# Two of four probability tiles transposed by VectorE and a trip through memory instead of TensorE

## The reference, cut to what matters

```python
        q = rmsnorm((hidden_states @ Wq).reshape(B, Sq, H, D), gq)      # H = 16 heads, D = 128
        k = rmsnorm((encoder_hidden_states @ Wk).reshape(B, Skv, H, D), gk)
        v = (encoder_hidden_states @ Wv).reshape(B, Skv, H, D)
        scores = jnp.einsum('bqhd,bkhd->bhqk', q, k) * scale
        attn = jax.nn.softmax(scores, axis=-1)                          # 512 x 512 for each (b, h)
        out = jnp.einsum('bhqk,bkhd->bqhd', attn, v)
        out = out.reshape(B, Sq, H * D) @ Wo
```

## Time and profile before

| What | us |
|---|---|
| Runs shown | 1462.48, 1463.65 (median), 1465.13 |
| Span of the profiled execution | 1461.5 |
| PE busy in that span | 1437.8 (98%) |
| DVE / ACT / POOL busy | 1107.0 / 977.5 / 864.5 |
| Packed steps, from the first y store to the last | 517.7 to 1223.0, 31 stores |

### The profile page before, as it was taken

How to read it: one execution, slowest core, us unless ns; L and a number is a source line. 1 busy time by engine, 2 the same in 40 slices (tenths; PEclk the granted TensorE clock), 3 DMA queues, 4 the chain that set the end, 5 groups by cost and what they waited for, 6 DMA issues and landing times.

```text
span 1461.5 us, 23763 instructions
## 1 busy us (share of the span) xinstructions
PE 1437.8 (98%) x8086; PEld 1223.0 (84%) x8086; DVE 1107.0 (76%) x2100; ACT 977.5 (67%) x2224; POOL 864.5 (59%) x701
## 2 busy tenths in 40 slices
PE   8999999999999999999999999999999999999998
PEld 6778788888888888888888888888888888888887
DVE  7888777777777777777777777777777776787777
ACT  7864477777776667667676767667676765666664
POOL 4785555555554566666575757575666655664341
PEclk9999999999999999999999999999999999999999
DMA  8420011111111333434333433433434331321002
GB/s 325 159 66 16 22 44 45 57 44 44 44 44 44 139 124 126 149 108 147 124 129 127 139 123 127 139 117 132 136 115 144 125 126 36 107 82 37 8 1 87
DMA packets 55495, 142.74 MB, mean 98 GB/s; under 512 B 5392, under 2 KB 5392, under 8 KB 55376
## 3 DMA queue, kind: packets, MB, share of 16 engines
q1 hardware_dynamic: 51616, 128.90, 26.1%
q0 software_dynamic: 3760, 12.32, 3.0%
HBM read 126.79 MB, written 14.42 MB: 97 GB/s over the span
## 4 chain that ended last, share of the span: by engine, by line
PE 82%; DVE 7%; ACT 4%; POOL 4%; issue 2%; DMA 0%; ACTq 0%; SPq 0%; DVEq 0%; POOLq 0%
PE w_bank L505 10%; PE w_bank L507 10%; PE w_bank L506 10%; PE j_bank L505 9%; PE j_bank L507 9%; PE j_bank L506 9%; PE t_bank L573 7%; PE s_bank L505 4%; PE s_bank L507 4%; PE s_bank L506 4%; PE t_bank L538 2%; POOL q_scale L1855 2%; POOL wo_lo L1815 2%; ACT prob L927 1%; PE t_bank L657 1%
## 5 line engine op out<-in xcount | busy, mean ns | idle before, releaser
L927 ACT ACTIVATE prob<-s_bank,neg_bias,q_scale 128x512 f32<-128x512 f32 x255 | 198.0, 777 | 186.5 <-DVE neg_bias L1422 186.4
L1262 DVE TENSOR_TENSOR probT_lo<-t_bank,probT_hi 128x512 fp32r<-128x512 f32 x260 | 176.4, 689 | 168.4 <-ACT probT_hi L892 168.4
L1476 DVE SCALAR_TENSOR_TENSOR x_sb<-w_bank,inv_sum,x_sb 128x512 f32<-128x512 f32 x254 | 188.4, 744 | 0.0
L1401 DVE TENSOR_REDUCE neg_max<-s_bank 128x1 f32<-128x512 f32 x255 | 168.6, 682 | 0.9 <-PE s_bank L507 0.9
L1815 POOL TENSOR_TENSOR xnT_lo<-xnT_raw,xnT_hi 128x512 fp32r<-128x512 f32 (+2 forms) x47 | 126.5, 2693 | 61.5 <-ACT xnT_hi L892 61.5
L573 PE MATMUL t_bank<-ident,prob 128*128 128x128 f32 x1008 | 151.4, 273 | 1.3 <-ACT prob L927 1.1
L892 ACT CAST probT_hi<-t_bank 128x512 fp32r<-128x512 f32 x260 | 150.1, 590 | 1.8 <-PE t_bank L515 1.8
L1855 POOL TENSOR_TENSOR q_scale<-q_ss,minus_half 128x4 f32<-128x4 f32 x64 | 65.9, 1030 | 143.6 <-DVE q_ss L1414 143.6
L505 PE MATMUL j_bank<-wkv_lo,cT_hi 128*128 128x256 f32 x512 | 145.1, 283 | 0.7 <-DVE oT_lo L1262 0.4
L507 PE MATMUL j_bank<-wkv_hi,cT_lo 128*128 128x256 f32 x512 | 144.6, 282 | 0.0
L506 PE MATMUL j_bank<-wkv_hi,cT_hi 128*128 128x256 f32 x512 | 144.4, 282 | 0.0
(11 more groups left out here) (308 smaller groups left out, 4454.2 us busy)
## 6 DMA issues: line engine op xcount, KB each, us to landing
stage<-w SPq DMA_DIRECT2D x96, 256.0 KB, 3.4
xnT_raw<-w_gu SPq DMA_DIRECT2D x31, 704.0 KB, 4.8
cT_raw<-w_gu SPq DMA_DIRECT2D x31, 704.0 KB, 4.7
xnT_raw<-w_dn SPq DMA_DIRECT2D x16, 768.0 KB, 4.4
cT_raw<-w_dn SPq DMA_DIRECT2D x15, 768.0 KB, 4.7
planes<-bits SPq DMA_DIRECT2D x16, 512.0 KB, 4.8
y<-stage SPq DMA_DIRECT2D x31, 256.0 KB, 4.0
x_sb<-x SPq DMA_DIRECT2D x5, 1024.0 KB, 10.9
```

Of the source, the lines that this page charges most:

```text
L927: nc.scalar.activation(prob[:, i, :], score_bank(t, i)[:], ACT.Exp, bias=neg_bias[:, u % 2, i:i + 1], scale=q_scale[:, u % 2, i:i + 1], ac ...
L1262: return nc.vector.tensor_tensor(dst, src, hi, ALU.subtract)
L1401: nc.vector.tensor_reduce(neg_max[:, u % 2, i:i + 1], score_bank(t, i)[:], AX_X, ALU.max, negate=True).then_inc(own_max, 1)
L1476: nc.vector.scalar_tensor_tensor(out=here, in0=w_bank[0][:] if packed else out_bank(t, i)[:], scalar=inv_sum[:, w % 2, i:i + 1], in1=here, ...
```

## The change

In the 31 packed steps tiles 0 and 1 of item u go another way. `softmax(0)` and `softmax(1)` write their keys in another order (32 columns of each 128-key block together). `turn_quads` (DVE) transposes both tiles in place in blocks of 32x32, one instruction over 128 x 1024. `move_pair` (SP) stores the pair to a DRAM scratch of 512 KB, waits for that store, and issues four loads of 128 KB that bring it back to `prob` with the blocks in their transposed places, in runs of 128 elements (512 B). `moved_hi` (ACT) and `moved_lo` (DVE), one instruction each over 128 x 1024, make the high and low part. Eight transposes on PE, two `probs_hi` and two `probs_lo` drop out of each packed step. For all steps the columns of `probT` hold keys in blocks of 32, which `values()` reads back with a stride (16 runs of 32 elements). `squares_out` moves ahead of `rows_to_lo` and `copy_y` in DVE's list. The semaphore counts follow (`TILES`, `MOVES`).

```diff
--- before.py
+++ after.py
@@ -123,7 +123,24 @@
+QUAD = 32
...
+def moved(u):
+
+    return 0 <= u < NI and T0 <= u + 1 < T0 + NB
...
+def turned_tiles(u):
+
+    return (2, 3) if moved(u) else range(NT)
+
+
+TILES = [sum(len(turned_tiles(v)) for v in range(u)) for u in range(NI + 1)]
+MOVES = [sum(moved(v) for v in range(u)) for u in range(NI + 1)]
...
+        probT_keys = [t[:, :, :].rearrange("p i s -> p (i s)").rearrange("p (q j c) -> p j q c", j=NT, c=QUAD)
+                      for t in probT]
...
+            def move_pair(u):
+
+                if not moved(u):
+                    return
+                sp.wait_ge(p_quads, MOVES[u] + 1)
+                wait(sp, p_moved, 16 * NT * MOVES[u])
+                sp.dma_start(turn_dram.rearrange("i p m -> p i m"), prob_pair).then_inc(p_stored, 16)
+                sp.wait_ge(p_stored, 16 * (MOVES[u] + 1))
+                for c in range(NT):
+                    sp.dma_start(prob[c * QUAD:(c + 1) * QUAD, 0:2, :].rearrange("a i (r m) -> a (i r) m", r=NT),
+                                 turn_dram.rearrange("i (r a) (c m) -> c a (i r) m", r=NT, c=NT)[c]).then_inc(p_moved, 16)
@@ -479,6 +526,7 @@
                     query_weights(SET[t] + 1)
                 if t >= H + 2 and fresh(t - 2):
                     out_weights(SET[t - 2] + 1)
+                move_pair(t - 1)
                 if 0 <= b < NB - 1:
                     e = expert(b + 1)
                     gate_up_weights(b + 1, 0, e)
@@ -532,8 +580,10 @@
                 if t == 1:
                     need(pe, q_ss_out, 1, 0, 1)
+                elif moved(t - 1):
+                    need(pe, q_ss_out, 1, t - 1, 1)
                 elif t:
-                    need(pe, p_lo, 4, t - 1, 2)
+                    wait(pe, p_lo, TILES[t - 1] + 2)
@@ -561,14 +611,17 @@
                 def probs(i):
                     if not score:
                         return
+                    if i not in turned_tiles(u):
+                        return
                     need(pe, p_exp, 4, u, i + 1)
...
@@ -577,21 +630,24 @@
                 def values():
                     if not value:
                         return
-                    need(pe, p_lo, 4, w, 4)
+                    wait(pe, p_lo, TILES[w + 1])
+                    wait(pe, pair_lo, MOVES[w + 1])
...
-                        last = product(j_bank[0][:], [a[:, w % 2, 1, j * P:(j + 1) * P] for a in kv],
-                                       [a[:, j, :] for a in probT], j == 0, j == NT - 1)
+                        last = product(j_bank[0][:].rearrange("p (q c) -> p q c", c=QUAD),
+                                       [a[:, w % 2, 1, j * P:(j + 1) * P] for a in kv],
+                                       [a[:, j] for a in probT_keys], j == 0, j == NT - 1)
...
@@ -923,17 +979,32 @@
                     need(act, s_max, 4, u, i + 1)
-                    need(act, p_turned, 4, u - 1, i + 1)
-                    nc.scalar.activation(prob[:, i, :], score_bank(t, i)[:], ACT.Exp,
+                    if i in turned_tiles(u - 1):
+                        wait(act, p_turned, TILES[max(u - 1, 0)] + list(turned_tiles(u - 1)).index(i) + 1 if u else 0)
+                    else:
+                        wait(act, pair_lo, MOVES[u])
+                    dst, src = prob[:, i, :], score_bank(t, i)[:]
+                    if i not in turned_tiles(u):
+                        dst = dst.rearrange("p (r j c) -> p j r c", j=NT, c=QUAD)
+                        src = bank_keys(score_bank(t, i))
+                    nc.scalar.activation(dst, src, ACT.Exp,
...
+                def moved_hi():
+                    if not moved(u):
+                        return
+                    act.wait_ge(p_moved, 16 * NT * (MOVES[u] + 1))
+                    need(act, pv_mm, 1, w, 1)
+                    copy_hi(probT_pair(0), prob_pair).then_inc(pair_hi, 1)
@@ -1153,6 +1224,7 @@
                 gate_tanh(1)
                 if packed:
                     key_hi()
+                    moved_hi()
                     query_hi()
...
+                def turn_quads():
+                    if not moved(u):
+                        return
+                    need(dve, p_exp, 4, u, 2)
+                    flat_pair = prob_pair.rearrange("p i s -> p (i s)")
+                    nc.vector.transpose(flat_pair, flat_pair).then_inc(p_quads, 1)
+
+                def moved_lo():
+                    if not moved(u):
+                        return
+                    dve.wait_ge(pair_hi, MOVES[u] + 1)
+                    lower(probT_pair(1), prob_pair, f32(probT_pair(0))).then_inc(pair_lo, 1)
@@ -1625,9 +1711,9 @@
                     gate_up_lo()
+                    squares_out()
                     rows_to_lo()
                     copy_y()
-                    squares_out()
                     inverses()
                     values_lo()
                     shift(0)
@@ -1662,20 +1748,20 @@
                 if packed:
+                    turn_quads()
                     inner(0)
-                    probs_lo(0)
                     maximum(2)
                     shift(2)
                     second_rows()
                     add(0)
                     maximum(3)
                     shift(3)
-                    probs_lo(1)
                     add(1)
                     probs_lo(2)
                     inner(1)
                     key_lo()
                     add(2)
+                    moved_lo()
                     query_lo()
                     inner_lo()
                     add(3)
```

More of the change, by code:

```diff
@@ L204, in flamingo_kernel, with probT_tile, probT_pair @@
         block_expert = sb("block_expert", [P, NBW], I32)
+        probT_keys = [t[:, :, :].rearrange("p i s -> p (i s)").rearrange("p (q j c) -> p j q c", j=NT, c=QUAD)
+                      for t in probT]
+        def probT_tile(part, i):
+            return probT[part][:, i, :].rearrange("p (r j c) -> p j r c", j=NT, c=QUAD)
+        def probT_pair(part):
+            return probT[part][:, 0:2, :]
+        prob_pair = prob[:, 0:2, :]
         def squares(t):
@@ L320, in flamingo_kernel @@
             sem("s_mm"), sem("s_max"), sem("p_exp"), sem("p_turned"), sem("p_hi"), sem("p_lo"))
+        p_quads, p_stored, p_moved, pair_hi, pair_lo = (
+            sem("p_quads"), sem("p_stored"), sem("p_moved"), sem("pair_hi"), sem("pair_lo"))
         late_normed, late_turned, late_hi, late_lo = (
@@ L583, in values @@
                     for j in range(NT):
-                        last = product(j_bank[0][:], [a[:, w % 2, 1, j * P:(j + 1) * P] for a in kv],
-                                       [a[:, j, :] for a in probT], j == 0, j == NT - 1)
+                        last = product(j_bank[0][:].rearrange("p (q c) -> p q c", c=QUAD),
+                                       [a[:, w % 2, 1, j * P:(j + 1) * P] for a in kv],
+                                       [a[:, j] for a in probT_keys], j == 0, j == NT - 1)
                     last.then_inc(pv_mm, 1)
                 def last_values(half):
-                    here = slice(half * S // 2, (half + 1) * S // 2)
-                    need(pe, p_lo, 4, w, 2 + 2 * half)
+                    here = slice(half * S // 2 // QUAD, (half + 1) * S // 2 // QUAD)
+                    wait(pe, p_lo, TILES[w] + 2 + 2 * half)
                     need(pe, v_lo, 1, w, 1)
                     for j in range(NT):
-                        last = product(value_bank(half), [a[:, w % 2, 1, j * P:(j + 1) * P] for a in kv],
-                                       [a[:, j, here] for a in probT], j == 0, j == NT - 1)
+                        last = product(value_bank(half).rearrange("p (q c) -> p q c", c=QUAD),
+                                       [a[:, w % 2, 1, j * P:(j + 1) * P] for a in kv],
+                                       [a[:, j, here] for a in probT_keys], j == 0, j == NT - 1)
                     last.then_inc(pv_mm, 1)
@@ L661, in table @@
                     pe.wait_ge(place_ready, 1 + NT)
-                    need(pe, p_lo, 4, 0, 4)
+                    wait(pe, p_lo, TILES[1])
                     for c in range(PAIRS):
@@ L933, in probs_hi @@
                         return
-                    need(act, p_turned, 4, u, i + 1)
-                    copy_hi(probT[0][:, :, i * P:(i + 1) * P],
-                            prob_bank(t, i)[:].rearrange("p (j q) -> p j q", j=4)).then_inc(p_hi, 1)
+                    if i not in turned_tiles(u):
+                        return
+                    wait(act, p_turned, TILES[u] + list(turned_tiles(u)).index(i) + 1)
+                    copy_hi(probT_tile(0, i), bank_keys(prob_bank(t, i))).then_inc(p_hi, 1)
+                def moved_hi():
[4 more added lines that the diff above has]
+                    copy_hi(probT_pair(0), prob_pair).then_inc(pair_hi, 1)
                 def values_hi():
@@ L1446, in probs_lo @@
                         return
-                    need(dve, p_hi, 4, u, i + 1)
```

(17 more changed lines are left out.)

8 lines of the change are left out of this document (6 added, 2 removed).

## The result

The changed kernel takes 1574.56 us (median of 4 runs, 1573.41 to 1577.35) against 1463.16 us of the kernel before: ratio 1.0761, 95% interval 1.0746 to 1.0776. It is 111 us slower; the prediction said 79 us (1542 us), in a range from 1468 to 1600.

A forecast was written before the change was run, and what follows sets the result against it. PE's work was taken to bound the kernel, with the step-end hand-over close behind. 1463.65 + 50 (late trip, PE's saving swallowed) + 28 (lower clock) = 1541.65, put at 1542 us; range 1468 to 1600.

The forecast's parts named there:

- PE's saving of 0.90 us: On PE behind the softmax: two groups of four transposes drop out, 0.45 us each, 28 us over 31 steps.
- (1) The DVE transpose: turn_quads starts at the end of tile 1's softmax on idle DVE and takes 1.22 us, at most 2.4.
- (2) to (4) The trip: Store behind down weights, four loads, weight loads ahead in the queue: blocks back at 932.7, between 931.2 and 934.2.
- The other estimate in the prediction: Skill page's 2.0 us plus bytes at 436 GB/s per DMA: store 3.2 us, load 2.3, kernel time 1511 us.
- the case of the run count: The four loads limited by their 1024 runs of 512 B instead of bytes: 10 us; not taken.
- (5) The hand-over: moved_hi, moved_lo, then qT_lo in sequence after the blocks return: 3.05 us; next scores(0) 1.63 us later, +50 us.
- The clock, 28 us: PE's clock falls after the 2.9 us wait, costing 1.2 us in three steps of four, 0.9 a step.
- full clock after waits of 3 us: Sign in the profile after that would prove the prediction wrong: PE keeps its full clock behind such waits.
- Moving `squares_out` costs nothing: On DVE it only permutes contiguous work of the same length; the softmax still waits for values_lo: zero cost.
- hidden trip: Rival: blocks back by 930.75, ACT and DVE do not wait, -0.36 us a step, 1453 us; chance 0.10.
- break-even time: Blocks' return at 931.07, 9.9 us after the softmax's end, where gain and loss cancel; chance 0.03 for landing near it.
- The strided reads: Value matmuls reading probT in 32-element runs might halve their pace: 2.8 us a step, 1628; chance 0.12 with other unseen costs.

The follow-up runs named there:

- e5: Changed kernel with eight extra 512-column matmuls ahead of scores(0) in each packed step, filling PE's wait for qT_lo: 1528.20 us, ratio 1.0440.
- e3: Changed kernel without the store and four loads, so the cast waits only for the 32x32 transposes and blocks stay unmoved: 1539.28 us, ratio 1.0512.
- e4: Changed kernel, trip unchanged, with the pair's cast moved behind query_squares and its subtraction behind add(3), both out of the hand-over: 1494.61 us, ratio 1.0211.
- e1: Changed kernel with squares_out put back behind copy_y on DVE, nothing else: 1576.28 us, ratio 1.0768.
- e11: Changed kernel, pair's subtraction behind add(3), copy_y and inverses behind shift(1), pair's cast out of the hand-over but ahead of query_squares: 1445.44 us, ratio 0.9883.
- e10: Changed kernel, trip included, with GpSimd's down_lo cut in four instructions, nothing else: 1575.18 us, ratio 1.0757.
- e7: Changed kernel without the store and loads (blocks not put in their places), with GpSimd's down_lo cut in four instructions: 1469.78 us, ratio 1.0031.

## Why the prediction was right, and where it was off

The direction, the place and the two mechanisms held: the trip ends behind the hand-over, `qT_lo` stands behind `moved_lo`, PE waits, and its clock falls after the wait. By the table the 111 us are the second part's 62, some 39 of lower clock (e5) and some 13 of the first part at full clock (11.03 us in e5 against 10.62), which together come to 114; the prediction had 50, 28 and nothing. That the forecast held is luck in one respect: it put the second part at 12.93 + 1.63 = 14.56 us, and half a microsecond below lay a floor of 14.08 (e3) that it did not see. By the prediction's own steps:

- **PE's saving of 0.90 us.** Right in size: e4's second part is 1.02 under before. In the changed kernel it is swallowed, as said.
- **(1) The DVE transpose**, taken at 1.22 us from its neighbours: 1.245 in all 31.
- **(2) to (4) The trip.** Back 11.51 us after S by the sum; the cast starts 11.82 after S in the mean. Store and down weights together are right: the store lands 7.5 us after S, by the sum at 927.9 and the 0.7 of the weight loads 7.4. The sum's upper value for the store (928.4) was given without a working. The other estimate in the prediction, a fixed 2.0 us and the bytes, gave 3.2 us for the store and 1511 us for the kernel (added up again its P is 931.6 and not 931.7, which is 3 us of the time); with 1.5 us of weights ahead of it the store would take 4.7, and it took 6.2 in the median. The loads, costed by their bytes at 2.7 us, land in 2.7 in the median, also in runs of 512 B, so the case of the run count is out:

```profile
prob<-turn SPq DMA_DIRECT2D x124, 128.0 KB, 2.7
```

- **(5) The hand-over**, 3.05 us: 3.03 from the blocks' return to the first scores. The second part grew by 1.99 instead of 1.63, 62 us instead of 50. Of the gap of 0.36, 0.31 are the later return, and 0.07 that I took 12.93 for the step I read, where the mean of 30 is 12.86. With the lower clock the steps came to 27.1 us in the mean, 25.4 to 28.8, where 25 to 27 were expected.
- **The clock, 28 us.** I took 1.2 us in three steps of four, 0.9 a step. It was 12.28 - 11.03 = 1.25 us a step against e5, that is 1.5 in each of 25 of 30 steps, 39 us. With the filler in its place 46 us came back, since the second part gave some 11 as well. The 1.2 came from a stretch that began a microsecond before the clock fell, so it held only part of the loss. Three steps of four was a guess: the length of the wait does not settle what the clock does. In the changed kernel it stayed full behind waits of 2.0 to 2.8 us and fell behind others of 2.0 to 4.4; in e3, with waits of 1.7 to 2.2 us, it fell in 19 of 30 steps. The sign "full clock after waits of 3 us" did not appear.
- **"Moving `squares_out` costs nothing"** was the wrong step. The order of contiguous work on one engine was not neutral: `q_scale` on GpSimd came earlier, GpSimd's next long instruction then met `inv_sum`, which took 1.13 us instead of 0.23 in two steps of three and put the first part at 11.03 instead of 10.62 in the mean. Undoing it gave nothing back (e1), because the blocks then came no earlier. So the nothing that the prediction put down for the time came out, but not for its reason: the trip covered the loss.
- **The rival "hidden trip", 1453 us**, did not come about, and its number was wrong as well. It costed the subtraction over the pair at 1.22 us wherever it stood. With the trip gone it would have met GpSimd's `down_lo` and given 1539 (e3). Its break-even time for the blocks' return did not exist in this order: 14.08 us is the least second part however early they are back. The chance of 0.10 that I gave it was too high.
- **The strided reads** cost next to nothing: the twelve matmuls of the values take 2.84 us from the first start to the next product's (842.43 to 845.27 in the step before the one shown) where they took 2.73 (915.13 to 917.86), 0.11 us a step or 3 us in all, an estimate from one step of each kernel. No halved pace.
- **TensorE or the other way for the transposes.** Where the result was wanted at once the other way lost 7.6%; where only the values waited for it and VectorE's order was changed too (e11), it won 1.2%.

GpSimd's instruction has little part in the 1.99 us of the second part: it holds 6 of the 31 subtractions, whose mean over all is 1.30 us instead of 1.23, 2 us in all, and e10 gains nothing that can be told from noise. Two things stay open: why the blocks are back 0.40 us earlier with full clock (e5), and what decides whether the clock falls behind a wait of some 2 us.

## What to carry to other kernels

Before work is put on an idle engine, read what stands behind it in that engine's list: of the 111 us that the change cost, 80 went away when two instructions no longer stood ahead of `query_hi` and `query_lo` (e4, still 2.1% slower than before), and with VectorE's and ScalarE's order fitted to it as well it became a gain of 1.2% (e11). When a wait is removed and little comes back, look for a second floor under it and remove both in one run. The two kinds of VectorE instruction that read only SBUF and met GpSimd here (the subtraction over the pair, the scalar operation on `inv_sum`) had no fixed price; cut GpSimd's long instructions, or keep the two apart. And before any gain from a reordering is counted, check in the trace whether GpSimd's instructions move with it.

## What the runs showed of the hardware

- A VectorE subtraction with two SBUF inputs (128x1024) took 1.23 us alone and up to 2.93 beside a GpSimd instruction of 3.5 us, ending 1.08 to 1.09 us after it in all 31 cases (e3). With GpSimd's work cut in four (4.92 us in all instead of 3.50) it took 1.42 in the median, waiting included (e7). A 128x4 scalar operation went from 0.23 to 1.13 us in the same way, ending 0.03 us after GpSimd's instruction. Subtractions of 0.69 us that read a bank kept it beside GpSimd (252 in the kernel before).
- After waits of 2.0 to 4.4 us PE's granted clock fell to 0.50, that is 1.2 GHz, in 25 of 30 steps, and such a step lost 1.5 us in the mean. Behind waits of 1.7 to 2.2 us it fell in 19 of 30 (e3). Eight matmuls in the wait kept it at 1.00 (e5).
- A DVE transpose of 32x32 blocks over 128x1024 float32 takes 1.245 us. A load of 128 KB in runs of 512 B, four in a row, lands 2.7 us after its issue in the median, no later than one of 256 KB in rows of 2 KB in the same run (3.0).
